# A transformer kernel on one core: the last but one query projection issued one step earlier, ahead of the first scores

## What is computed

```python
e = leaky_relu(attn_self[:, :, None] + attn_neigh[:, None, :]) + MASK_VAL * (1.0 - adj)
out = elu(einsum('hnm,hmo->hno', softmax(e), feat) + b)              # two such layers
...
q = apply_rope(rmsnorm((h @ q_w.T).reshape(B, S, Hq, hd), q_norm_w), cos, sin)
k = apply_rope(rmsnorm((h @ k_w.T).reshape(B, S, Hkv, hd), k_norm_w), cos, sin)
scores = where(causal, einsum('bhqd,bhkd->bhqk', q, k) * scale, finfo.min)
hidden = hidden + (softmax(scores) @ v) @ o_w.T
...
return hidden + moe_out
```

## Time and profile before

| | |
|---|---|
| median of 3 runs | 645.02 us (644.83 to 646.51) |
| profiled execution | 646.5 us, its span 644.7 us |
| PE busy | 602.9 us, 94% of the span |
| DVE busy | 438.5 us, 68% |
| POOL busy | 295.6 us, 46% |
| ACT busy | 268.2 us, 42% |
| mean granted clock of PE | 0.979 |
| chain that ended last | PE 68%, DVE 18%, POOL 5%, issue 5%, ACT 3%, DMA 1% |

### The profile page before, as it was taken

The page is one execution under the profiler, slowest core; times in us unless marked ns, Lnnn a source line. Parts: engine busy times, 40 slices in busy tenths (PEclk is TensorE's granted clock), DMA queues, the critical chain, the costliest instruction groups (busy, mean ns, idle before and its releaser), DMA issues.

```text
span 644.7 us, 10312 instructions
## 1 busy us (share of the span) xinstructions
PE 602.9 (94%) x3253; PEld 433.8 (67%) x3253; DVE 438.5 (68%) x1286; ACT 268.2 (42%) x653; POOL 295.6 (46%) x576
## 2 busy tenths in 40 slices
PE   5988889899999999799999998799999998999998
PEld 2555536586789745587779764588679874676886
DVE  5878579667387679866287759866558746654463
ACT  2425065466333046466333136456434214574020
POOL 1718168864241348864232148874323047762000
PEclk9999998899999999999999999979999998999999
DMA  8910000000000000000000000000000000000000
GB/s 292 384 56 3 17 4 2 0 2 1 2 0 2 17 18 4 1 2 1 2 1 2 18 16 1 2 2 1 2 0 2 2 17 0 2 0 2 1 1 17
DMA packets 8729, 14.41 MB, mean 22 GB/s; under 512 B 908, under 2 KB 7372, under 8 KB 8420
## 3 DMA queue, kind: packets, MB, share of 16 engines
q1 hardware_dynamic: 8676, 13.76, 6.1%
HBM read 12.70 MB, written 1.05 MB: 21 GB/s over the span
## 4 chain that ended last, share of the span: by engine, by line
PE 68%; DVE 18%; POOL 5%; issue 5%; ACT 3%; DMA 1%; DVEq 0%; POOLq 0%; SPq 0%; ACTq 0%
PE bank L596 15%; PE bank L494 11%; PE ob L468 7%; PE bank L554 6%; PE bank L573 4%; PE tb L457 4%; PE bank L540 3%; DVE tt L937 3%; DVE ssq L1006 2%; PE bank L618 2%; PE bank L569 2%; PE bank L565 2%; DVE lr L928 2%; PE zb L449 2%; DVE m L1003 2%
## 5 line engine op out<-in xcount | busy, mean ns | idle before, releaser
L772 POOL TENSOR_SCALAR tt<-tt,gmn 128x256 f32<-128x256 f32 x128 | 81.6, 649 | 50.1 <-DVE gmn L937 49.5
L540 PE MATMUL bank<-wqkv_sb,hT 128*128 128x512 f32 x192 | 93.8, 625 | 0.8 <-ACT v_sb L680 0.8
L704 ACT ACTIVATE prob<-bank,sneg,rms 128x128 f32<-128x128 f32 (+1 forms) x128 | 64.0, 508 | 68.6 <-DVE sneg L1035 68.3
L494 PE MATMUL bank<-m,wgu_sb 128*128 128x128 f32 (+1 forms) x480 | 86.6, 330 | 0.7 <-DVE early L1082 0.6
L815 POOL TENSOR_TENSOR m<-early,rope_s 128x256 f32<-128x256 f32 x80 | 72.0, 923 | 29.5 <-ACT early L685 29.3
L831 POOL TENSOR_SCALAR prob<-prob,srcp 128x128 f32<-128x128 f32 (+1 forms) x128 | 54.2, 441 | 55.4 <-DVE srcp L1106 55.3
L494 PEld LDWEIGHTS bank<-m,wgu_sb 128*128 128x128 f32 x480 | 71.2, 191 | 8.6 <-DVE early L1082 2.0
L468 PEld LDWEIGHTS ob<-feat,gpT 128*128 128x128 f32 x512 | 63.7, 195 | 0.9 <-issue 0.5
L928 DVE SCALAR_TENSOR_TENSOR lr<-zs 128x512 f32<-128x512 f32 x64 | 49.8, 780 | 21.0 <-ACT zs L663 19.2
L468 PE MATMUL ob<-feat,gpT 128*128 128x33 f32 x512 | 63.6, 269 | 0.1
L554 PE MATMUL bank<-kT,qT 128*128 128x128 f32 (+1 forms) x256 | 62.3, 360 | 0.9 <-ACT prob L704 0.9
(11 more groups left out here) (161 smaller groups left out, 1069.9 us busy)
## 6 DMA issues: line engine op xcount, KB each, us to landing
wqkv_sb<-wqkv_dram SPq DMA_DIRECT2D x1, 3072.0 KB, 11.5
wgu_sb<-wgu_dram SPq DMA_DIRECT2D x2, 1408.0 KB, 10.9
wo_sb<-wo_dram SPq DMA_DIRECT2D x1, 2048.0 KB, 17.3
wd_sb<-wd_dram SPq DMA_DIRECT2D x1, 1408.0 KB, 15.8
xin<-x_dram SPq DMA_DIRECT2D x4, 256.0 KB, 2.8
out_dram<-rows SPq DMA_DIRECT2D x8, 128.0 KB, 1.7
rows<-gat_rows_dram SPq DMA_DIRECT2D x2, 256.0 KB, 2.9
cin<-ctxT_dram SPq DMA_DIRECT2D x4, 64.0 KB, 2.8
```

Source lines behind the costliest of these rows:

```text
L494: mm = pe.matmul(ps[:, m * N + c0:m * N + c1], wgu_sb[:, m, k, n * P:(n + 1) * P], tokT[:, k, c0:c1], start=(k == 0), stop=(k == KT - 1))
L540: mm = pe.matmul(ps[:, :], hT[:, k, t * P:(t + 1) * P], wqkv_sb[:, k, c * G * HD:(c + 1) * G * HD], start=(k == 0), stop=(k == KT - 1))
L704: ins = act.activation(prob[:, n % 5, i * nk:(i + 1) * nk], ps[:, i * nk:(i + 1) * nk], ACT.Exp, bias=sneg[:, n, i:i + 1], scale=rq(g, t, ...
L772: ins = pool.tensor_scalar(tt[:, k % 3, h, :], tt[:, k % 3, h, :], -1.0, gmn[:, k % 3, h:h + 1], ALU.mult, ALU.add)
```

## The change

Entry 10 of `QKV_AT` is 10 and no longer 11. Query projection 10 (unit 8) then stands in step 10, behind projection 9 and ahead of turn 4 and score 0; step 11 keeps projection 11, turns 5 and 6 and score 1. All engines follow the same table, and the quick banks are dealt out anew in these two steps: projection 10 takes bank 2, turn 4 bank 3.

```diff
-QKV_AT = (1, 2, 3, 4, 5, 6, 7, 8, 9, 10, 11, 11)
+QKV_AT = (1, 2, 3, 4, 5, 6, 7, 8, 9, 10, 10, 11)
```

## The result

The changed kernel is slower: 655.64 us median (653.58 to 662.04, 4 runs) against 645.76 us (644.83 to 650.24, 4 runs) for the kernel before, a ratio of 1.0131 with a 95% interval of 1.0086 to 1.0175. The ratios in this document are those on record, over the executions in the fast state alone; they can differ from the quotient of the medians (here 1.0153) by up to 0.4%. The profiled execution has a span of 651.8 us against 644.7, and a mean granted clock of 0.966 against 0.979. PE works on the same 3253 instructions, but is busy for 610.1 us instead of 602.9.

What follows compares the result with a forecast made beforehand. DVE's and ACT's chain was taken to decide when TensorE, 94% busy, may go on. From 646.5 us: -1.0 for chains and batch 3, -1.5 for batch 2's lateness, +8.0 for low clock give 652.0 us, range 647.2 to 656.5.

Steps and rivals of the forecast that it cites:

- the 3.94 us stall: Before the change, TensorE's wait at turn 6 in batch 1 for ACT to empty projection 10's bank (L686).
- First stall: At turn 6, TensorE waits 1.4 us for GpSimd's unit 6 (L815) in place of 3.94 us for ACT.
- Second stall: After score 2, TensorE waits 5.1 us for ACT's gpT, queued behind score 1's exponentials, in place of 1.19 us.
- The sign that it gave: A wait of 4.5 to 5.5 us at L457 for ACT's L668 after score 2, in batches 0 to 2.
- Chains: DVE and ACT work up to score 1's exponentials and gpT: -0.3 us a batch, bounds 0 and -0.6.
- Clock: Half clock behind the wait after score 2 costs 2.7 us a batch in batches 0 to 2, bounds 0 and 4.7.
- Rival (a): Short cold stretches behind each moved stall: 0.8 to 1.7 us a batch, 646.4 to 649.1 us in all; chance 0.17.
- Batch 3: The batch without graph work beside it: -0.1 us, bounds -0.3 and 0.3.
- Batch 2's lateness of 1.5 us: Before, a long low-clock stretch made batch 2's gpT-fed transposes 1.54 us late; the change was to remove this.
- The sum: Profiled 646.5 us, -1.0 for chains and batch 3, -1.5 for batch 2's lateness, +8.0 for low clock: 652.0 us.
- (b): No charge for the clock: full speed behind the stall after score 2, 644.0 us, no change; chance 0.10.
- (c): Faster: gpT of step 12 ready when TensorE arrives after score 2, saving 2.5 us in three batches, 637.5 us; chance 0.08.

Runs made afterwards that it cites:

- the second measurement: The changed kernel run again without any edit: 657.85 us median, 1.0123 of the kernel before.
- the filled kernel: The changed kernel plus dummy matmuls where TensorE stands still, at turn 6 (batches 1, 2) and ahead of step 13's transposes (batches 0 to 2): 1.0006 of before.
- the filled kernels: The changed kernel plus dummy matmuls, either at turn 6 and ahead of step 13's transposes (1.0006 of before) or only ahead of step 13's transposes (0.9973).

## Why the prediction was right

The forecast of 652.0 us with a range of 647.2 to 656.5 held: the median is 655.64. The path is the one that it named: the 3.94 us stall moved behind score 2, and the cost is the half clock behind it.

*What is off in its readings.* ACT could not have emptied projection 10's bank "by 263": its four matmuls end at about 262.9 (261.11 + 1.76), and ACT's two instructions take 0.96 us, so 263.8 is the earliest. Nothing hangs on it. And it left out two falls of the kernel before: behind the first turn of batch 0, after a wait of 1.71 us (0.50 granted from 96.80 to 100.00), and behind that of batch 3, after 2.69 us (0.50 from 540.60 to 543.80). They were a sign that a wait shorter than 2.26 us can do it, and so that a first stall of 1.4 us might not keep the clock.

*First stall.* Forecast 1.4 us, with turn 6 at 267.1 in the time of before, 23.1 us behind the first turn; measured 1.94 us and 269.81 - 246.16 = 23.65 us. The cause named, POOL's unit 6, fits: it starts at 268.30, lasts 1.41 us and ends 0.10 us ahead of turn 6. What was missed is 0.5 us in POOL's last Newton step, which the moved pair on DVE now runs beside:

```profile
266.18 0.75 POOL L754 TENSOR_TENSOR rms<-rms,rms_a 128x16 f32<-128x16 f32 x1
267.09 0.20 POOL L801 TENSOR_SCALAR rms<-rms 128x16 f32<-128x16 f32 x1 [0.16 <-POOL rms L754]
268.30 1.41 POOL L815 TENSOR_TENSOR m<-early,rope_s 128x256 f32<-128x256 f32 x2
```

On DVE at this time stands the L1003 of unit 8, with two inputs in SBUF:

```profile
266.17 0.68 DVE L1003 TENSOR_TENSOR m<-early,rope_c 128x512 f32<-128x512 f32 x1
```

The same step took 0.22 us before. The Trainium skill's rule that a VectorE instruction with two SBUF inputs contends with a GpSimd instruction that reads SBUF (SBUF — State Buffer, "Who interferes with whom") agrees with this row. The prediction held it against DVE's L937 alone and did not ask what DVE's moved work does to POOL.

In the profiled execution the clock fell behind this first stall in batches 1 and 2. The prediction had it hold there, which it did in the second measurement.

*Second stall.* Forecast 5.1 us, measured 4.53 and 4.54 where the clock was up; the 0.5 us is the lateness of turn 6, the rest of the walk held. The sign that it gave, 4.5 to 5.5 us in batches 0 to 2, is met in all three batches of the second measurement but only in batch 0 of the first (then 2.98 and 0.56), where the low clock behind turn 6 hid the rest. Score 0's sneg came 0.56 us later behind the first turn, against 0.6 forecast, but not "against L801": L801 was late by 0.53 us itself.

*Chains.* Forecast -0.3 us a batch with bounds 0 and -0.6. The transposes of step 13 begin 34.16 us behind the first turn before (278.12 - 243.96) and 33.95 after (280.11 - 246.16): -0.21. The filled kernel says the same, 44.02 against 44.24. That the size fits is in part a cancellation. Both L937 of this step now took 0.95 and 0.94 us (0.94 and 0.41 before), the full growth that by the prediction's own sum leaves -0.05, and the L1003 of unit 9 took 1.20 us in place of 0.82. Against it L1012, which the prediction did not list, took 0.21 us in place of 0.67.

*Clock.* Forecast 2.7 us a batch. Over the 44.0 us of the filled kernel the changed stretches are longer by 2.3, 1.5 and 3.7 us, and in the second measurement by 3.1, 2.6 and 2.1: the means are 2.5 and 2.6. The mechanism was right, as the filled kernels show. That the size fits so closely is partly luck: the prediction averaged over low stretches of 3.4, 3.4 and 9.4 us behind the stall, and behind the second wait there were 6.6 to 6.8 us four times in six, 3.4 us once, and once the rest of 16.8 us that had begun behind turn 6. Rival (a), 0.8 to 1.7 us a batch, holds for one batch of six.

*Batch 3.* Forecast -0.1, measured 29.67 against 29.79 us. (In both kernels the clock fell behind the first turn of batch 3. In the two filled versions of the changed kernel it held there, and the same stretch took 28.1 us.)

*Batch 2's lateness of 1.5 us.* Right in place: 45.60 against 44.25 us. Whether the median of 645.02 us is the kernel without this lateness is not shown, as only one execution has a trace; as the kernel's usual time it is low. In a later comparison of 17 executions the median was 648.58, and all but one (654.41) lay between 644.65 and 650.42.

*The sum.* From trace to trace the time rose by 7.08 us (646.50 to 653.58), where the prediction had 5.5. The changed stretches of batches 0 to 2 give 2.09, 1.26 and 2.09 of it, 5.44 together, and batch 3 -0.12: what the prediction summed is right within 0.2 us. The rest is a fall in the expert products of batch 2, 1.64 us, which it did not have. The other 2.1 us to the median of 655.64 lie in executions without a trace. The clock also falls in places that no edit touches. In the twelve profiled executions it was low for 3.4 to 13.6 us before the first turn of batch 0, and this turn came between 94.9 and 100.1 us. That such falls are what spreads the times is likely, but was not measured.

The other rivals: (b), no charge for the clock, is what the filled kernel does artificially; unfilled, all six batches measured were charged 1.5 us or more. (c), faster, named the right point: the second wait. An edit of ACT's order does what the change could not.

## What to carry to other kernels

A stall that is removed at one wait is only worth what the next wait in the same queue leaves of it, so walk on to the next wait before counting. Where the clock falls behind a stall, the place of the stall matters more than its length: ahead of slack the low clock was free (batch 1 of the kernel before), ahead of the work that bounds the batch it cost a little under half of the work done in it (3.1 us for 6.80 in batch 0 of the second measurement, 1.5 for 3.40 in batch 1 of the first). Where two streams share an in-order queue, put the item whose operands are ready in front of the one that waits for a long chain.

## What the runs showed of the hardware

The granted clock did not always return after the same time of work: stretches at 1.2 GHz lasted 3.4 us, 6.8 us (after, measured again), 10.2 us (batch 2 of before) and 17 us (batch 2 of after, 421.20 to 438.00, in which PE was busy for 16.24 of 16.80 us). Why some are longer stays open. A wait of 1.46 us was followed by a lower clock once in three times, one of 1.96 us likewise.

Nor does it take a wait. In the changed kernel with both stalls filled the clock fell among the expert products of batch 0, with PE busy before and throughout:

```profile
190.00:195.00 5.00, 5.00 (x45) 1.00 0.00 0
195.00:202.00 7.00, 7.00 (x36) 0.51 0.00 0
```

The trace marks no wait of PE's between 129.04 and 241.24 us. The same happened in batch 2 of this kernel and of the changed one (499.6). What lowers the clock there is open; filling the stalls did not keep it from happening.
